# Edge stage of a two-layer graph network: ScalarE writes constants into the accumulators, a bias is moved out of the message, and edge attributes are scaled before they are turned

## The chip, the cores and the metric

The kernel runs on one core of one Trainium2 chip. The metric is the time on the device in microseconds (us), from the first to the last instruction of the core, as the median of several executions of the same program. A lower number is better.

## What is computed

The input is a graph with 50,000 nodes (128 features each) and 25,000 edges, sorted by their receiving node `dst`, with 128 attributes per edge. The reference, cut to what matters:

```python
h = maximum(layernorm(x), 0)
# layer 0 (PNA): a message per edge, four aggregates per receiving node
m = concat(h[dst], h[src]) @ W_pre.T + b_pre
mx, mn, mean, std = segment max, min, mean, sqrt(relu(var) + 1e-5) of m over dst   # 0 for nodes without edges
agg = concat(mx, mn, mean, std);  amp = log(deg + 1);  att = 1 / amp
x = x + (concat(h, agg, agg * amp, agg * att) @ W_post.T + b_post) @ W_lin.T + b_lin
# layer 1: mean of the edge attributes over the receiving node
h = maximum(layernorm(x), 0)
x = x + relu(concat(h, segment_mean(edge_attr)) @ W1 + b1) @ W2 + b2
```

## The kernel before, in words

**Two stages.** The node stage goes over all nodes in 98 chunks of 512 rows, computes every node as if it had no edges, stores the result, and writes a table of normalised rows and inputs to memory. The edge stage goes over the 25,000 edges in 49 chunks of 512, computes the nodes that do have edges, and writes only the last edge of each run of equal `dst` back over the stored row. Each stage is software-pipelined: every engine runs its own `edge_step(k)` in an order written out by hand, in which it works on chunk k ("have"), k+1 ("ahead") and k-1 ("behind"), and semaphores tie the engines together. An engine executes its own queue strictly in the written order, so a wait holds back all that is written behind it.

**Feature-major edges.** In the edge stage gathered rows are turned on TensorE, so that edges lie along the free dimension. A segmented sum, maximum or minimum is then one scan on VectorE over 512 edges, with a mask row that restarts it at each new receiver: `keep` (0 or 1, multiplied), `reset` and `lift` (added). The masks are made once, written to memory, and broadcast back to 128 partitions for each chunk by SyncE's queue.

**One edge step on each engine.**
- TensorE (PE in the profile): `turn_sender`, `layer0` for four tiles of 128 edges (L614 to L624, thirteen matmuls of up to 384 columns per tile, into the banks 5 and 6 in turn), `sender_part` (L670), `turn_receiver` (L650), `turn_normed` (L678), `turn_attr` (L661), `hidden` (L691 to L696), and `outputs`: one matmul of `ones` with `b2_rows` that puts the bias b2 into bank 7 (L701), then sixteen (by the records) with the hidden rows (L704).
- VectorE (DVE): four `mix` (L1100, L1106, L1115), five scans (L1170, L1184, L1198, L1208, L1218), the means and the variance (L1227, L1234, L1239), three `low_part` (L1122: a float32 value less its rounded high part), two more low parts (L1150, L1157), `moments`, `factors`, `outputs` (L1134).
- ScalarE (ACT): copies out of PSUM with Relu (L810, L816, L847, L865), `message` (L835: the product of `sender_part` in bank 3 plus the bias b_pre, into bank 4), its square (L841), high parts (L853), `normalise` (L824), `deviation` (L869, L873).
- GpSimd (POOL): the indirect transfers, that is, per chunk eight gathers (L444: senders `hs`, receivers `rows`, each for four tiles) and four scatters (L450); in addition three small copies of indices and factors (L397, L418, L438), three one-element additions that order the transfers (`go`, L465), and two wide operations: `receiver_const` (L406: the receiver's rows plus a constant, 128x512, into `xdc`) and `mean_attr` (L461: the running sum of attributes times 1/count, into `attr_mean`).

`attr_mean` of chunk k-1 is the operand of the first matmul of `hidden(k-1)` in TensorE's step k. SyncE loads the masks of chunk k+4 once `attr_mean` of chunk k exists.

Of the kernel before, what the change touches and what calls it, by code (L numbers as in the profile page):

```python
# [47 lines left out]
def build(nc, x, src, dst, edge_attr, w_pre, b_pre, w_post, b_post, w_lin, b_lin, w1, b1, w2, b2, out):  # L48
# [13 lines left out]
    keep_row = nc.dram_tensor("keep_row", [ROWS * RW], BF16, kind="Internal").ap()  # L62
    reset_row = nc.dram_tensor("reset_row", [ROWS * RW], BF16, kind="Internal").ap()
# [43 lines left out]
    edge_const = sb("edge_const", [P, TILES, P])  # L107
# [4 lines left out]
    PAIR, LOW = 64, 32  # L112
    ones = sb("ones", [PAIR, P], F32R)
    b2_hi = sb("b2_hi", [PAIR, CHUNK], F32R)
    b2_rows = sb("b2_rows", [PAIR, CHUNK], F32R)

    attr_mean = sb("attr_mean", [P, 2, CHUNK])
    hd_flat = attr_mean[:].rearrange("p b w -> p (b w)")  # L120
# [17 lines left out]
    inv_count = sb("inv_count", [P, RW])  # L138
    keep_sb = sb("keep_sb", [P, RW], BF16)
# [7 lines left out]
    scale = sb("scale", [P, 2, ROWS, 2])  # L147
# [36 lines left out]
    gather_go = sb("gather_go", [P, 1])  # L184
    oidx = sb("oidx", [P, 4, TILES], I32)
    amp_att = sb("amp_att", [P, 4, 2, TILES])
# [37 lines left out]
    TURNS = 4  # L224
# [31 lines left out]
    with nc.Block() as block:  # L256

        @block.sync
        def _(sp):
# [30 lines left out]
            def node_step(k, i):  # L290
                if k == 0:

                    sp.wait_ge(sem("masks_done"), 1)
                    sp.dma_start(keep_row.rearrange("(r w) -> r w", w=RW), keep_sb[0:ROWS, :]).then_inc(r, 16)
                    sp.dma_start(reset_row.rearrange("(r w) -> r w", w=RW), reset_sb[0:ROWS, :]).then_inc(r, 16)
                    sp.dma_start(lift_row.rearrange("(r w) -> r w", w=RW), lift_sb[0:ROWS, :]).then_inc(r, 16)
                    sp.dma_start(inv_row.rearrange("(r w) -> r w", w=RW), inv_count[0:ROWS, :]).then_inc(r, 16)
# [26 lines left out]
            def edge_step(k, i):  # L324
                c = k + 4
                if edge(c):
                    s = c % 4
                    if c == 0:
                        sp.wait_ge(r, 64)
                    if c >= 4:  # L330

                        sp.wait_ge(sem("e_attr_mean"), c - 3 + EU * i)
                    m = sem(f"e_masks_in{s}")
                    for dst_sb, row in ((keep, keep_row), (reset, reset_row), (lift, lift_row), (inv, inv_row)):
# [25 lines left out]
        def _(pool):  # L360
# [34 lines left out]
            def copy_scales(c, i):  # L395
                t = bass.ds(2 * c + (2 * EU) * i, 2)
                pool.tensor_copy(amp_att[:, c % 4].rearrange("p w (r h) -> p w r h", h=2), scale[:, :, t, :]).then_inc(sem("e_scale"), 1)  # L397

            def receiver_const(c, i):
                pool.wait_ge(sem(f"e_gathered{c % 4}"), 16 * 2 * TILES * (c // 4 + 1) + 16 * 2 * TILES * i)  # L400
                if c == 0:

                    pool.wait_ge(sem("n_x1"), NODE_CHUNKS)
                if c >= 2:
                    pool.wait_ge(sem("e_mixed"), TILES * (c - 1) + TILES * EU * i)
                pool.tensor_tensor(xdc[:, c % 2], xd[:, c % 4], edge_const[:], ALU.add).then_inc(sem("e_xdc"), 1)  # L406
# [13 lines left out]
            def gather_rows_of(c, i):  # L420
# [9 lines left out]
                if c >= 4:  # L430
# [5 lines left out]
                    pool.wait_ge(sem("e_xdc"), c - 3 + EU * i)  # L436
# [18 lines left out]
            def mean_attr(c, i):  # L455
                pool.wait_ge(sem("e_attr_run"), c + 1 + EU * i)
                if c >= 2:
                    pool.wait_ge(sem("e_u_psum"), 2 * (c - 1) + 2 * EU * i)
                if c < 4:
                    pool.wait_ge(sem(f"e_masks_in{c % 4}"), 64)  # L460
# [3 lines left out]
            def go():  # L464
                pool.tensor_tensor(gather_go[:], eps_col[:], eps_col[:], ALU.add)  # L465

            def edge_step(k, i):
                if edge(k + 1):
                    copy_scales(k + 1, i)
                if edge(k + 4):  # L470
                    gather_rows_of(k + 4, i)
                    pool.wait_ge(sem("e_idx"), k + 5 + EU * i)
                    go()
                    gather(k + 4, (0, 1))
                if edge(k + 1):
                    receiver_const(k + 1, i)
                if edge(k + 4):
                    if edge(k + 1):
                        pool.wait_ge(sem("e_xdc"), k + 2 + EU * i)
                        go()  # L480
                    gather(k + 4, (2, 3))
                if edge(k - 2):
                    scatter_rows_of(k - 2, i)
                    pool.wait_ge(sem("e_oidx"), k - 1 + EU * i)
                    go()
                    scatter(k - 2)
                if edge(k):
                    mean_attr(k, i)
# [6 lines left out]
        def _(pe):  # L495
# [42 lines left out]
            pe.wait_ge(sem("count_ready"), 1)  # L538
            for s in range(SCALERS):
# [3 lines left out]
            pe.wait_ge(sem("comb_h_out"), 1)  # L543

# [51 lines left out]
            def layer0(c, j, i):  # L596

                acc = bank[5 + j % 2]
                if c == 0 and j == 0:

                    pe.wait_ge(sem("n_out"), NODE_CHUNKS)
                if c == 0 and j == 1:
                    pe.wait_ge(sem("n_ut"), 2 * NODE_CHUNKS)
# [712 lines left out]
```

## Time and profile before

| | |
|---|---|
| time, median of 3 runs | 1620.67 us (1620.6 to 1627.65) |
| the profiled execution | 1626.46 us, of which the span of the core is 1624.7 us |
| TensorE busy | 1494.9 us (92% of the span) |
| VectorE busy | 1397.1 us (86%) |
| GpSimd busy | 1236.0 us (76%) |
| ScalarE busy | 939.8 us (58%) |
| mean granted TensorE clock | 0.973 of full speed |

The node stage fills the first 560 us or so, the edge stage the rest. A share of busy time is an average over both. Gaps between the instructions of an engine are not counted as busy, even where they recur before each instruction of one kind.

### The profile page before, as it was taken

How to read it: one execution, taken by the hardware profiler on the slowest of the kernel's cores; microseconds unless marked ns; L12 is line 12 of the kernel's file. 1: busy time of each engine (PE TensorE's matmuls, PEld its weight loads, DVE VectorE, ACT ScalarE, POOL GpSimd, SP SyncE). 2: the span in 40 equal slices, each digit the busy share in tenths (PEclk: the TensorE clock that was granted, in tenths of full speed). 3: DMA queues.
4: the chain of work that ended last, by engine and by line, in shares of the span. 5: the costliest groups of instructions: out<-in, count | busy, mean ns of one | idle time of the engine just before them, and what ended most of it. 6: DMA issues, size and time to landing. Idle time of an engine off the chain costs nothing.

```text
span 1624.7 us, 33700 instructions
## 1 busy us (share of the span) xinstructions
PE 1494.9 (92%) x8747; PEld 1257.4 (77%) x8747; DVE 1397.1 (86%) x4327; ACT 939.8 (58%) x1976; POOL 1236.0 (76%) x1376
## 2 busy tenths in 40 slices
PE   2899999999999759999999999999998999999995
PEld 2799998889999648888777787777777777777783
DVE  5899999999999468899888997988887888888892
ACT  1799999999999534455444453434444444444341
POOL 1778777777778777888888888888888888888833
PEclk9899999999999979999999999999999999999997
DMA  3455555555555622233233333333332323333200
GB/s 88 163 209 206 207 207 201 201 201 204 204 203 206 187 87 85 84 86 90 90 91 92 93 92 91 92 91 89 93 91 79 95 86 89 94 93 93 89 18 15
DMA packets 158898, 197.95 MB, mean 122 GB/s; under 512 B 18912, under 2 KB 115321, under 8 KB 158858
## 3 DMA queue, kind: packets, MB, share of 16 engines
q1 hardware_dynamic: 136906, 149.93, 28.3%
q0 software_dynamic: 21952, 47.55, 9.5%
q8 instruction: 17, 0.28, 0.1%
q14 instruction: 23, 0.19, 0.0%
HBM read 111.11 MB, written 90.17 MB: 124 GB/s over the span
## 4 chain that ended last, share of the span: by engine, by line
PE 82%; DVE 6%; issue 5%; ACT 3%; another core or an unknown queue 3%; DMA 1%; SPq 1%; POOL 0%; DVEq 0%; ACTq 0%; POOLq 0%
PE bank L572 12%; PE bank L621 6%; PE bank L581 6%; PE bank L614 5%; PE bank L691 5%; PE bank L618 5%; PE bank L615 5%; PE bank L624 5%; PE bank L704 5%; PE bank L670 3%; PE bank L593 3%; PE bank L591 3%; PE bank L592 3%; PE bank L555 3%
## 5 line engine op out<-in xcount | busy, mean ns | idle before, releaser
L444 POOL DMA_INDIRECT rows<-table,idx x196 | 208.3, 1063 | 59.7 <-issue 59.7
L450 POOL DMA_INDIRECT y<-nout,oidx x196 | 200.0, 1020 | 70.6 <-issue 70.3
L444 POOL DMA_INDIRECT hs<-table,idx x196 | 204.8, 1045 | 44.7 <-issue 31.2
L614 PE MATMUL bank<-comb_lo,agg_hi 128*128 128x384 f32 x588 | 212.4, 361 | 16.6 <-DVE nout L1019 10.7
L572 PE MATMUL bank<-w_sb,nut 128*128 128x128 f32 x1568 | 202.9, 283 | 5.5 <-issue 4.7
L379 POOL TENSOR_TENSOR runs<-nx,b_all 128x512 f32<-128x512 f32 x98 | 125.9, 1284 | 107.9 <-DVE nx L1029 107.8
L572 PEld LDWEIGHTS bank<-w_sb,nut 128*128 128x128 f32 x1568 | 184.5, 193 | 23.1 <-issue 14.2
L618 PE MATMUL bank<-comb_hi,agg_lo 128*128 128x384 f32 x588 | 200.1, 340 | 0.0
L615 PE MATMUL bank<-comb_hi,agg_hi 128*128 128x384 f32 x588 | 199.5, 339 | 0.0
L781 ACT ACTIVATE nh<-nx,nms,nrs 128x128 f32<-128x128 f32 x392 | 161.8, 484 | 1.1 <-DVE nms L1002 0.5
L621 PE MATMUL bank<-comb_sd,agg_sd 128*128 128x384 f32 x392 | 159.6, 489 | 0.0
L865 ACT ACTIVATE nut<-bank,b_col 128x512 f32<-128x512 f32 x98 | 67.5, 689 | 151.9 <-PE bank L696 138.4
L391 POOL TENSOR_SCALAR rows<-rows,nmv,nrs 128x128 f32<-128x128 f32 x196 | 154.6, 798 | 0.0
L388 POOL TENSOR_TENSOR xdc<-rows,lone_const 128x512 f32<-128x512 f32 x98 | 125.1, 1276 | 32.7 <-DVE nrs L1039 32.7
L691 PE MATMUL bank<-attr_mean,w_attr 128*128 128x512 f32 x196 | 111.3, 652 | 30.9 <-issue 30.2
L796 ACT ACTIVATE nut<-bank,b_col 128x512 f32<-128x512 f32 x196 | 125.6, 681 | 15.3 <-remote 11.2
L1100 DVE SCALAR_TENSOR_TENSOR part<-bank,amp_att,xdc 128x128 f32<-128x128 f32 x196 | 67.6, 345 | 75.8 <-remote 27.1
L614 PEld LDWEIGHTS bank<-comb_lo,agg_hi 128*128 128x128 f32 x588 | 111.3, 189 | 20.5 <-issue 14.8
L624 PE MATMUL bank<-comb_h_lo,hdt 128*128 128x384 f32 x196 | 125.0, 638 | 0.0
L810 ACT ACTIVATE hst<-bank 128x512 f32<-128x512 f32 x49 | 29.3, 598 | 164.2 <-PE bank L637 130.5
L615 PEld LDWEIGHTS bank<-comb_hi,agg_hi 128*128 128x128 f32 x588 | 111.6, 190 | 2.2
L618 PEld LDWEIGHTS bank<-comb_hi,agg_lo 128*128 128x128 f32 x588 | 111.1, 189 | 0.0
(180 smaller groups left out, 4196.9 us busy)
## 6 DMA issues: line engine op xcount, KB each, us to landing
table<-rows SPq DMA_DIRECT2D x98, 512.0 KB, 2.7
rows<-in_x SPq DMA_DIRECT2D x98, 256.0 KB, 3.1
y<-nout SPq DMA_DIRECT2D x98, 256.0 KB
inv<-inv_row SPq DMA_DIRECT2D x49, 256.0 KB
attr<-in_edge_attr SPq DMA_DIRECT2D x48, 256.0 KB
keep<-keep_row SPq DMA_DIRECT2D x49, 128.0 KB
reset<-reset_row SPq DMA_DIRECT2D x49, 128.0 KB
lift<-lift_row SPq DMA_DIRECT2D x49, 128.0 KB
```

The source lines that it names most:

```text
L379: pool.tensor_tensor(nx1b[:, c % 4], nx1[:, c % 2], b2_all[:], ALU.add).then_inc(sem("n_x1b"), 1)
L391: last = pool.tensor_scalar(nh[:, c % 4, j, :], nx[:, c % 4, j, :], nmv1[:, c % 4, j, 0:1], nrs1[:, c % 4, j:j + 1], ALU.subtract, ALU.mult)
L444: pool.indirect_dma_start(out=to[:, s, j, :], out_offset=None, in_=of, in_offset=bass.IndirectOffsetOnAxis(ap=idx[:, s, which, j:j + 1], a ...
L450: pool.indirect_dma_start(out=out, out_offset=bass.IndirectOffsetOnAxis(ap=oidx[:, c % 4, j:j + 1], axis=0), in_=eout[:, c % 2, j, :], in_ ...
L572: mm = pe.matmul(bank[5][:, j * P:(j + 1) * P], nut[:, c % 2, m, j * P:(j + 1) * P], w2_sb[:, m, :], start=(m == 0), stop=(m == 1))
L614: pe.matmul(acc[:, 0:SCALERS * P], hi, w_lo, start=(a == MX), stop=False, skip_group_check=True)
L615: pe.matmul(acc[:, 0:SCALERS * P], hi, w_hi, start=False, stop=False, skip_group_check=True)
L618: pe.matmul(acc[:, 0:SCALERS * P], lo, w_hi, start=False, stop=False, skip_group_check=True)
L621: pe.matmul(acc[:, 0:SCALERS * P], agg_sd[:, c % 2, cols], comb_sd[:].rearrange("p s f -> p (s f)"), start=False, stop=False, skip_group_c ...
L624: mm = pe.matmul(acc[:, 0:SCALERS * P], h[:, c % 2, cols], w[:].rearrange("p s f -> p (s f)"), start=False, stop=(w is comb_h_hi and h is ...
L691: pe.matmul(bank[b][:], w1_attr[:, cols], attr_mean[:, c % 2, :], start=True, stop=False)
L781: last = act.activation(nh2[:, b, j, :], nx1[:, b, j, :], ACT.Identity, scale=nrs2[:, b, j:j + 1], bias=nms2[:, b, j:j + 1])
```

## The change

- **Seeds.** `acc_seed` (128x384) holds all constants of layer 0. ScalarE copies it into the accumulator (bank 5 or 6) ahead of each tile (`seed`, four per chunk), and TensorE's first matmul of the tile accumulates onto it. One opening matmul per bank precedes the stage (`open_sums`). `receiver_const` and `xdc` go: `mix` reads the gathered row itself.
- **Output bias.** ScalarE copies b2 into bank 7 (`out_bias`). TensorE's matmul with `ones` goes.
- **Message.** b_pre no longer enters the message; it is multiplied by the summed weights once, in the setup, and is part of `acc_seed`. `message` on ScalarE goes; the products alternate between the banks 3 and 4, and scans and square read them there. The scans wait for the square (`e_bsq`).
- **Attributes.** ScalarE multiplies each edge's attributes by 1/count before they are turned (`scale_attr`, four 128x128 per chunk), and the scan uses a float32 mask `keepm` = (count-1)/count, so that it yields a running mean. `mean_attr` on GpSimd goes; `hidden` reads the scan's result. The new mask is one more broadcast of 256 KB per chunk.
- **Moves.** The `low_part` of the maximum moves from VectorE to GpSimd. GpSimd gathers three chunks ahead instead of four. On VectorE the receiver's low part comes first, the scans change places, and the attributes' scan goes from the middle of the step to behind the last `mix`. TensorE turns the receiver first, and the attributes one tile sooner; ScalarE has another order.

The core of the diff (conditions and the renamed counters of masks left out):

```diff
 POOL
-            def receiver_const(c, i):
-                ...
-                pool.tensor_tensor(xdc[:, c % 2], xd[:, c % 4], edge_const[:], ALU.add).then_inc(sem("e_xdc"), 1)
-            def mean_attr(c, i):
-                ...
-                pool.tensor_tensor(attr_mean[:, c % 2, :], run_attr[:, c % 2, :], inv[:, c % 4, :],
-                                   ALU.mult).then_inc(sem("e_attr_mean"), 1)
+            def low_part(a, rows, c, i):
+                pool.wait_ge(sem(f"e_hi{a}"), c + 1 + EU * i)
+                if c >= 2:
+                    pool.wait_ge(sem("e_layer0"), TILES * (c - 1) + TILES * EU * i)
+                pool.tensor_tensor(agg_lo[:, c % 2, a, :], rows, agg_hi[:, c % 2, a, :],
+                                   ALU.subtract).then_inc(sem(f"e_lo{a}"), 1)
 gather_rows_of(c, i), for c >= 4:
-                    pool.wait_ge(sem("e_xdc"), c - 3 + EU * i)
+                    pool.wait_ge(sem("e_mixed"), TILES * (c - 3) + TILES * EU * i)
 edge_step(k, i):
-    copy_scales(k + 1); gather_rows_of(k + 4); gather(k + 4, (0, 1)); receiver_const(k + 1)
-    gather(k + 4, (2, 3)); scatter(k - 2); mean_attr(k)
+    gather_rows_of(k + 3); gather(k + 3, (0, 1)); copy_factors(k + 2)
+    gather(k + 3, (2, 3)); scatter(k - 2); low_part(MX, run_max[...], k + 1)

 PE
             def layer0(c, j, i):
-                if j >= 2:
-                    pe.wait_ge(sem("e_mixed"), TILES * c + j - 1 + TILES * EU * i)
-                elif c >= 1:
-                    pe.wait_ge(sem("e_mixed"), TILES * (c - 1) + j + 3 + TILES * EU * i)
+                pe.wait_ge(sem("e_seeded"), TILES * c + j + 1 + TILES * EU * i)
-                    pe.matmul(acc[:, 0:SCALERS * P], hi, w_lo, start=(a == MX), stop=False, skip_group_check=True)
+                    pe.matmul(acc[:, 0:SCALERS * P], hi, w_lo, start=False, stop=False, skip_group_check=True)
 outputs(c, i):
-                pe.matmul(bank[7][:], ones[:], b2_rows[:], start=True, stop=False, skip_group_check=True)
+                pe.wait_ge(sem("e_b2"), c + 1 + EU * i)
 edge_step(k, i):
-    turn_sender(k + 1); layer0(k, 0); sender_part(k + 1); turn_receiver(k + 1); layer0(k, 1)
-    turn_normed(k - 1); layer0(k, 2); turn_attr(k); hidden(k - 1); layer0(k, 3); outputs(k - 1)
+    turn_receiver(k + 1); turn_sender(k + 1); layer0(k, 0); sender_part(k + 1); layer0(k, 1)
+    turn_attr(k); turn_normed(k - 1); layer0(k, 2); hidden(0, k - 1); hidden(1, k - 1); layer0(k, 3); outputs(k - 1)

 ACT
-                act.activation(bank[4][:], bank[3][:], ACT.Identity, bias=b_pre_col[:]).then_inc(sem("e_b"), 1)
+            def seed(c, j, i):
+                if c == 0 and j < 2:
+                    act.wait_ge(sem("e_sums_open"), 1)
+                elif j >= 2:
+                    act.wait_ge(sem("e_mixed"), TILES * c + j - 1 + TILES * EU * i)
+                else:
+                    act.wait_ge(sem("e_mixed"), TILES * (c - 1) + j + 3 + TILES * EU * i)
+                act.activation(bank[5 + j % 2][:, 0:SCALERS * P], acc_seed[:], ACT.Copy).then_inc(sem("e_seeded"), 1)
+            def scale_attr(c, i):
+                ...
+                for j in range(TILES):
+                    last = act.activation(attr[:, c % 2, j, :], attr[:, c % 2, j, :], ACT.Copy,
+                                          scale=factor[:, c % 4, 2, j:j + 1])
+            def out_bias(c, i):
+                act.wait_ge(sem("e_ut"), 2 * c + 1 + 2 * EU * i)
+                act.activation(bank[7][:], b2_all[:].rearrange("p j f -> p (j f)"), ACT.Copy).then_inc(sem("e_b2"), 1)
 edge_step(k, i), after:
+    seed(k, 1); sender_turned(k + 1); receiver_turned(k + 1); spread(k - 1); message_squared(k + 1)
+    normalise(k - 1); seed(k, 2); normed_turned(k - 1); mean_squared(k + 1); high_part(MX, k + 1)
+    hidden(0, k - 1); seed(k, 3); hidden(1, k - 1); high_part(ME, k + 1); out_bias(k - 1)
+    high_part(MN, k + 1); seed(k + 1, 0); variance_pos(k + 1); deviation(k + 1); scale_attr(k + 1)

 DVE edge_step(k, i), after:
+    outputs(k - 2); factors(k - 1); receiver_low(k + 1); mix(k, 0); scan_sum(k + 1); scan_max(k + 1)
+    message_mean(k + 1); normed_low(k - 1); mix(k, 1); scan_squares(k + 1); scan_min(k + 1)
+    square_mean(k + 1); mix(k, 2); variance(k + 1); low_part(ME); low_part(MN); mix(k, 3)
+    scan_attr(k); moments(k)
```

The setup gains the mask `keepm`, the product of b_pre with the summed weights, the two instructions that make `acc_seed`, and a reciprocal of the turned factors (98 edge half-rows by two); it loses the splitting of b2 and one reciprocal of 98x256.

## Rows read from the trace of the kernel before

**Rows 1.** The page: busy time of each engine, its share of the span, instructions.

```profile
PE 1494.9 (92%) x8747; PEld 1257.4 (77%) x8747; DVE 1397.1 (86%) x4327; ACT 939.8 (58%) x1976; POOL 1236.0 (76%) x1376
```

**Rows 2.** Busy us of each engine by stretch; then granted clock, DMA share, GB/s.

```profile
976.00:1520.00 544.00, 507.77 (x2584) 409.01 (x2585) 455.77 (x951) 239.54 (x456) 445.46 (x512) 0.98 0.32 91
1529.80:1581.00 51.20, 51.02 (x257) 41.28 (x258) 46.42 (x97) 21.76 (x41) 24.55 (x28) 0.97 0.14 42
```

**Rows 3.** The two longest waits of GpSimd, 640 to 1520 us: in total, times, longest.

```profile
POOL y L450 <- issue: 60.8, 168, 0.6
POOL rows L444 <- issue: 50.9, 167, 0.3
```

**Rows 4.** Timeline of GpSimd: the first instruction of four of its edge steps.

```profile
626.24 0.65 POOL L397 COPY amp_att<-scale 128x8 f32<-128x8 f32 x1
...
668.54 0.22 POOL L397 COPY amp_att<-scale 128x8 f32 x1
...
688.04 0.24 POOL L397 COPY amp_att<-scale 128x8 f32 x1
...
1529.80 0.21 POOL L397 COPY amp_att<-scale 128x8 f32<-128x8 f32 x1
```

**Rows 5.** Waits of TensorE, 640 to 1520 us.

```profile
PE bank L691 <- issue: 28.2, 18, 2.2
PE bank L678 <- ACT nh L824: 15.8, 14, 2.0
```

**Rows 6.** Groups of GpSimd, 640 to 1520 us: count, busy, mean ns, idle before.

```profile
L444 POOL DMA_INDIRECT rows<-table,idx x167 | 179.8, 1077 | 50.9 <-issue 50.9
L444 POOL DMA_INDIRECT hs<-table,idx x167 | 176.4, 1056 | 37.4 <-issue 25.3
L461 POOL TENSOR_TENSOR attr_mean<-runs,inv 128x512 f32<-128x512 f32 x42 | 54.6, 1300 | 0.4
L406 POOL TENSOR_TENSOR xdc<-rows,edge_const 128x512 f32<-128x512 f32 x42 | 54.4, 1294 | 0.7
```

**Rows 7.** Timeline of TensorE near the end: the bias matmul of two steps.

```profile
1556.83 0.49 PE L701 MATMUL bank<-b_rows,ones 64*128 64x512 f32 x1
1557.25 2.05 PE L704 MATMUL bank<-w_sb,nut 128*128 128x128 f32 x16
...
1575.99 0.49 PE L701 MATMUL bank<-b_rows,ones 64*128 64x512 f32 x1
```

**Rows 8.** Timeline of VectorE and of GpSimd: instructions of both at once.

```profile
1017.57 2.06 DVE L1227 TENSOR_TENSOR mean_b<-runs,inv 128x512 f32<-128x512 f32 x1
1017.78 1.29 POOL L461 TENSOR_TENSOR attr_mean<-runs,inv 128x512 f32<-128x512 f32 x1
...
1042.15 0.69 DVE L1239 TENSOR_TENSOR var<-var,mean_b 128x512 f32<-128x512 f32 x1
1042.25 1.51 POOL L444 DMA_INDIRECT hs<-table,idx  x1
```

**Rows 9.** Groups of ScalarE, 640 to 1520 us.

```profile
L824 ACT ACTIVATE nh<-nx,ms,rs 128x128 f32<-128x128 f32 x168 | 68.9, 486 | 0.0
L835 ACT ACTIVATE bank<-bank,b_pre_col 128x512 f32<-128x512 f32 x42 | 27.8, 662 | 100.1 <-PE bank L670 87.2 <-issue 9.2 <-remote 3.8
```

**Rows 10.** Group of VectorE, 640 to 1520 us.

```profile
L1122 DVE TENSOR_TENSOR agg_lo<-runs,agg_hi 128x512 fp32r<-128x512 f32 x86 | 62.8, 770 | 0.0
```

**Rows 11.** TensorE's end of a tile, and VectorE's first reading of it.

```profile
1074.83 0.34 PE L624 MATMUL bank<-comb_h_hi,hdt 128*128 128x384 f32 x1
...
1076.96 0.35 DVE L1100 SCALAR_TENSOR_TENSOR part<-bank,amp_att,xdc 128x128 f32<-128x128 f32 x1 [3.16 <-remote]
```

**Rows 12.** Timeline of TensorE: one of its waits on `hidden`.

```profile
1061.82 1.15 PE L691 MATMUL bank<-attr_mean,w_attr 128*128 128x512 f32 x2 [2.08 <-issue]
```

**Rows 13.** The stretch that begins there, with the columns of Rows 2.

```profile
1061.80:1066.60 4.80, 4.78 (x10) 2.85 (x11) 4.66 (x7) 0.69 (x1) 4.27 (x5) 0.64 0.45 140
```

**Rows 14.** Timeline of VectorE in the setup: the reciprocal that goes.

```profile
23.37 1.70 DVE L963 RECIPROCAL runs<-runs 98x256 f32<-98x256 f32 x1
```

More of the change, by code:

```diff
@@ L538, in _ @@
             pe.wait_ge(sem("count_ready"), 1)
+            pe.matmul(bank[6][:, P:(1 + SCALERS) * P], b_pre_wide[:], part_sum[:].rearrange("p s f -> p (s f)"),
+                      start=True, stop=True)
             for s in range(SCALERS):
@@ L626, in layer0, with open_sums @@
                 mm.then_inc(sem("e_layer0"), 1)
+            def open_sums():
+                pe.wait_ge(sem("n_out"), NODE_CHUNKS)
+                pe.wait_ge(sem("n_ut"), 2 * NODE_CHUNKS)
+                for acc in (bank[5], bank[6]):
+                    mm = pe.matmul(acc[:, 0:SCALERS * P], ident[:], comb_sd[:].rearrange("p s f -> p (s f)"),
+                                   start=True, stop=True, skip_group_check=True)
+                mm.then_inc(sem("e_sums_open"), 1)
             def turn_sender(c, i):
@@ L676, in turn_normed @@
                     pe.wait_ge(sem("e_h2l"), c + EU * i)
+                if not last:
+                    pe.wait_ge(sem("e_hst"), c + 3 + EU * i)
                 for j in range(TILES):
@@ L875, in edge_step @@
             def edge_step(k, i):
-                ahead, behind = edge(k + 1), edge(k - 1)
+                have, ahead, behind = edge(k), edge(k + 1), edge(k - 1)
+                if k == 0:
+                    seed(0, 0, i)
+                if have:
+                    seed(k, 1, i)
                 if ahead:
                     sender_turned(k + 1, i)
+                    receiver_turned(k + 1, i)
                 if behind:
@@ L881, in edge_step @@
                 if ahead:
-                    message(k + 1, i)
-                    receiver_turned(k + 1, i)
+                    message_squared(k + 1, i)
                 if behind:
                     normalise(k - 1, i)
-                if ahead:
-                    message_squared(k + 1, i)
+                if have:
+                    seed(k, 2, i)
                 if behind:
@@ L1264, in edge_step @@
                     factors(k - 1, i)
+                if ahead:
+                    receiver_low(k + 1, i)
                 if have:
@@ L1278, in edge_step @@
                     scan_squares(k + 1, i)
+                    scan_min(k + 1, i)
                     square_mean(k + 1, i)
-                    variance(k + 1, i)
-                if have:
-                    scan_attr(k, i)
-                if ahead:
-                    low_part(MX, run_max[:, (k + 1) % 2, :], k + 1, i)
-                    low_part(MN, run_min[:, (k + 1) % 2, :], k + 1, i)
                 if have:
```

244 lines of the change are left out of this document (126 added, 118 removed).

## The prediction

> **What bounds the kernel now.** I read the page first [rows 1]: TensorE is busy for 92% of the span, which makes it the suspect. The change is in the edge stage, so I asked for the busy time by stretch [rows 2]. From 976 to 1520 us TensorE is busy for 507.8 of 544 us, VectorE for 455.8, GpSimd for 445.5, ScalarE for 239.5. GpSimd's 82% looks harmless. Its waits say otherwise [rows 3]: from 640 to 1520 us it waits for nothing but "issue", never over 0.6 us, about 0.3 us ahead of each transfer. Those gaps belong to the transfers, so GpSimd is never idle for want of work. Its timeline gives the pace [rows 4]: from the first of these starts to the last are 43 steps, (1529.80 - 626.24) / 43 = 21.01 us each.
>
> TensorE does wait [rows 5]: 28.2 us in 18 waits ahead of `hidden`, whose operand `attr_mean` GpSimd makes, and 15.8 us in 14 waits for `normalise`. The wait of 2.08 us before 1061.82 [rows 12] ends at the moment GpSimd's wide operation does. What TensorE can do unhindered stands near the end, when no gathers are left: 1575.99 - 1556.83 = 19.16 us a step [rows 7]. So GpSimd at 21.0 us sets the pace, TensorE at 19.2 us comes next. VectorE has 455.8 / 544 x 21.3 (the mean step in that stretch, by GpSimd's starts) = 17.8 us of work, ScalarE by the same sum 9.4.
>
> **The change part by part, per edge step.**
>
> GpSimd. `receiver_const` goes: 54.4 / 42 = 1.30 us [rows 6]. `mean_attr` goes, another 1.30 us, and `low_part` of the maximum comes, the same kind of operation (two 128x512 inputs, one output); I give it the same 1.30 us. Twelve transfers and the small copies stay; the copy of factors has twelve elements a row for eight, nothing that shows. Sum: 21.01 - 1.30 = 19.7 us. The unknown is how much of the 21.01 is mutual hindrance with VectorE. A gather takes 1.06 to 1.08 us on the mean [rows 6], and 1.51 us where a VectorE operation on two buffers runs beside it [rows 8]. The quickest step of all took 688.04 - 668.54 = 19.5 us [rows 4], so hindrance is worth 1.5 us of the mean step. One such VectorE operation leaves VectorE (the low part), the order of the rest changes. Bounds for GpSimd: 19.5 - 1.3 = 18.2 us with next to no hindrance; above, 20.2 us, one third more hindrance than now. I take 19.7, the hindrance as it is, since that quickest step stands alone among the 43.
>
> A rule of the Trainium skill bears on this (SBUF — State Buffer, "Who interferes with whom"): a VectorE instruction with two inputs in SBUF contends with a GpSimd instruction that reads SBUF, and the later one waits until the first is through. The trace agrees for wide operations: `mean_b` took 2.06 us beside GpSimd's 1.29 us [rows 8], against the 0.69 us that a like operation, `variance`, takes in the same rows. By the same section such an operation should not hold up the making of descriptors; the 1.51 us of the gather [rows 8] speaks against that. By the rule alone GpSimd would come near the lower bound, and the pace would be TensorE's.
>
> TensorE. The bias matmul of `outputs` goes: 1557.25 - 1556.83 = 0.42 us [rows 7], so 19.16 - 0.42 = 18.74 us. Nothing else leaves it. This is its best case. In many steps its work ends later than recorded: a tile ends at 1075.17, VectorE could read it at once and starts at 1076.96 [rows 11], 1.8 us late, where others start 0.2 us behind the recorded end. Over 45 steps the extra lateness at this place has a mean of 0.7 us, from 0 to 2.4; if TensorE truly spends it, it needs 19.4 us. That still fits under 19.7.
>
> VectorE. One `low_part` goes, 0.77 us [rows 10], two wide GpSimd operations become one beside it. 17.8 becomes 17.0 us. `mix` costs the same with the gathered row. Not the pace.
>
> ScalarE. Out: `message`, 0.66 us. In: four seeds (128x384; between 0.49 for 128x128 and 0.66 for a 128x512 that is written into a bank [rows 9], so 2.0 to 2.6 us), `out_bias` 0.66, `scale_attr` four like `normalise`'s, 68.9 / 42 = 1.64 us. Sum: 9.4 - 0.66 + 4.3 to 4.9, up to 13.6 of 19.7 us. Not the pace, but it now stands between VectorE and TensorE: `layer0` waits for a seed where it waited for `mix`. I walked through a step with TensorE's durations, t = 0 at `turn_receiver`. Tile 0 ends at 3.7, the sender's product at 4.6, the square at 5.3, `normalise` at 7.0, seed 2 at 7.5; TensorE wants them at 7.8 and 8.3. `hidden(0)` is copied by 13.4, seed 3 done at 13.9, wanted at 14.2. The bias is in bank 7 at 16.2, wanted at 17.0. Everything fits, seed 3 with 0.3 us. What slips is covered by 19.7 - 18.74 = 0.96 us of slack a step; with the cover gone each us slipped costs a us.
>
> New waits. `low_part(MX, k+1)` is GpSimd's last item in step k and gates `layer0(k+1, 0)`. In the other direction GpSimd's step k waits for chunk k-1 to be mixed. The loop runs over two steps: from the gate 15.8 us of TensorE to the end of tile 3, 1.1 us of `mix`, 19.7 us of GpSimd, 36.6 in all, 18.3 a step, below the pace. Behind GpSimd's wait stand gathers needed two steps later, and scatters. If it fails, `low_part` is late next, and with it the whole of TensorE's step. With a lead of three chunks a gather still has over a step to land. SyncE queues five mask loads for four, one of them 256 KB, behind a wait for the attributes' scan; they are needed three steps later, and DMA engines are 32% busy [rows 2]. The attributes of chunk k+2 queue behind them and have some 17 us. I cost both at nothing.
>
> Outside the steady part. Start: the first `mix` results no longer wait behind low parts, about -3 us. The last four steps, in which TensorE leads: 4 x 0.42 = -1.7. Setup: a reciprocal of 98x256 goes (1.70 us [rows 14]), the splitting of b2 goes beside TensorE's work, and `acc_seed`, a reciprocal of about 1.3 us and a matmul come ahead of the node stage; I take +2.5 (bounds 0 and +4). The node stage is untouched.
>
> Sum: 43 x (21.01 - 19.7) = 56.3, + 3 + 1.7 - 2.5 = 58.5 us less. The profiled execution would fall from 1626.5 to 1568; it lies 5.8 us above the median of the runs, so for the median 1620.7 - 58.5 = 1562 us.
>
> **The rivals.**
>
> (a) *TensorE sets the pace.* Hindrance on GpSimd nearly vanishes in the new order, GpSimd needs 18.2 us. TensorE's best is 18.74, say 18.9: 43 x 2.11 = 91, + 2.2 = 93 less, 1528 us. For it: the quickest GpSimd step, and TensorE steps of 19.16 us. Against: the mean gather is well above its shortest, and TensorE's lateness of 0.7 us. The skill's section named above speaks for it.
>
> (b) *GpSimd was not what held TensorE.* Its unbroken row is what it takes up when TensorE is slow for reasons of its own (lateness, or the clock: behind the 2.08 us wait the granted clock was 0.64 over 4.8 us [rows 12, 13]). Then only the matmul is saved, 0.42 x 49 = 20.6 us: 1600 us. For it: some TensorE steps take 23 us although its waits in them are 2 us. Against: GpSimd has no wait.
>
> (c) *The change does not do what it says:* ScalarE's handoffs eat the gain. If seeds and bias come late by a mean 1.5 us a step, TensorE needs 18.74 + 0.7 + 1.5 = 20.9, 4.7 us less over 43 steps, and 2.2 outside: 1614 us, no change that can be told. Against: the walk through a step above.
>
> (d) *Slower.* TensorE waits for seed 2 and seed 3 each step, 0.5 us each, and its clock falls once a step. The fall cost 0.36 x 4.8 = 1.7 us in [rows 13]. 18.74 + 1.0 + 1.7 = 21.4 us, 43 x 0.4 = 17 more: 1638 us. It decides once waits and falls exceed 21.01 - 18.74 = 2.27 us a step. For it: seed 3 has 0.3 us of slack. Against: a single wait of 2 us was needed for the fall before, and some such waits had none behind them.
>
> **How the numbers follow.** The forecast (GpSimd at 19.2 to 20.2 us a step, 1541 to 1584 us) has a chance of 0.56. (a) 0.12, (b) 0.17, (c) 0.08, (d) 0.07. A difference of 0.5%, 8 us, is about what a measurement of this kernel can tell from none. Below 1612.6: the forecast, (a) and nearly all of (b), 0.84. Within: the rest of (b) and (c), 0.09. Above 1628.8: (d), 0.07. The predicted time is 1562 us. The range, 1530 to 1604, takes in the forecast, most of (a) and (b), and leaves out (c) and (d).
>
> **What would show it.** GpSimd's starts 19.7 us apart and still without waits but "issue"; if it waits for `mix` or for the high part, TensorE has taken over (a). TensorE's waits move from `hidden` to the third matmul of tile 0, which needs GpSimd's low part; if they stand ahead of the first matmul of tiles 2 or 3, released by ScalarE, (c) or (d) holds. L701 is gone, and `sender_part`, tiles and `hidden` keep their durations. ScalarE's busy time a step rises to 13 to 14 us, VectorE's falls by some 0.8. In the setup TensorE's first node matmul comes 0 to 4 us later than at 40.6 us. The prediction is wrong if GpSimd's gathers stretch more than before with the new order of scans, if ScalarE's copies into a bank cost much more than its copies out of one, or if TensorE's unexplained lateness was what set the pace.

## The result: 9.3% slower where it was measured, 5.7% faster in other series

The changed kernel took 1782.47 us (median of 4 runs, 1770.21 to 1784.44) against 1620.63 us for the kernel before (4 runs, 1619.68 to 1627.65): the ratio is 1.093, 95% interval 1.0835 to 1.1027. A further run of it is on record with 1757.25 us. I had predicted 1562 us, range 1530 to 1604, and 0.84 for faster. On that measurement the prediction is wrong.

That number can't be understood without this: in a later series the same file, unedited, took a median of 1535.21 us (4 runs, 1534.34 to 1535.57) against 1627.55, ratio 0.943, interval 0.9414 to 0.9446. The kernel before shows no such jump (medians 1620 to 1631 throughout). A series is a set of kernels run one after another on one chip (a "call" in the expectations). I name the two conditions *late* (TensorE's signals come late) and *prompt*; all runs of a series agreed. The result and series 1, 3 and 6 were late, 2, 4 and 5 prompt; series 1 and 2 had the same chip, 23 minutes apart (there I know the condition from edited kernels, since the unedited one was in neither).

The page's busy time, of the changed kernel, in the late condition and then in the prompt one:

```profile
PE 1519.1 (86%) x8704; PEld 1270.6 (72%) x8704; DVE 1338.9 (76%) x4275; ACT 1060.3 (60%) x2368; POOL 1114.7 (63%) x1329
```
```profile
PE 1451.2 (95%) x8704; PEld 1242.0 (81%) x8704; DVE 1311.9 (86%) x4275; ACT 1057.9 (69%) x2368; POOL 1137.0 (74%) x1329
```

The sums move by 5% at most, so the time is in waits. One stretch of the edge loop, late, by windows (the columns are those of [rows 2]), then its waits:

```profile
640.00:1440.00 800.00, 678.19 (x3338) 543.64 (x3336) 562.89 (x1200) 398.64 (x866) 491.62 (x637) 0.94 0.31 89
```
```profile
engine line waited for: us in total, times, longest us
ACT nh2t L846 <- remote: 168.6, 31, 6.8
POOL idx L437 <- DVE nx L1148: 165.9, 32, 8.2
...
PE bank L697 <- issue: 92.7, 33, 3.8
...
ACT bsq L840 <- remote: 63.8, 15, 4.7
...
PE bank L605 <- ACT bank L873: 13.7, 12, 2.8
```

and the same stretch, prompt:

```profile
640.00:1440.00 800.00, 790.42 (x4225) 659.09 (x4224) 682.79 (x1516) 502.13 (x1099) 637.36 (x803) 1.00 0.39 114
```
```profile
ACT nut L864 <- PE bank L701: 130.1, 84, 2.6
ACT bsq L840 <- PE bank L672: 117.6, 42, 3.3
...
ACT nh2t L846 <- PE bank L682: 48.7, 43, 1.2
```

Late, 3338 TensorE rows fit into 800 us; prompt, 4225 do. GpSimd no longer sets the pace in the late condition: it waits 5 us a step for the mix. What leads there is the wait of ScalarE's copy of h2, the normalised rows that TensorE has turned (nh2t), 5.4 us a time, and its releaser is "remote": at the moment of release no recorded instruction ends. Prompt, TensorE and GpSimd are nearly level. GpSimd waits for "issue", as in [rows 3], and for the mix only 3.0 us in all, and TensorE's third matmul of tile 0 waits for GpSimd's low part in every step, at its weight load and in some steps at the matmul:

```profile
POOL y L449 <- DVE nx L1148: 3.0, 10, 0.3
PEld bank L609 <- POOL agg_lo L459: 23.0, 42, 1.0
PE bank L609 <- POOL agg_lo L459: 7.5, 11, 0.7
```

One step shows the wait for h2. Late:

```profile
1138.14 0.66 PE L682 MATMUL bank<-ident,nh 128*128 128x128 f32 x4 [0.58 <-issue]
...
1144.74 2.07 PE L697 MATMUL bank<-runs,w_attr 128*128 128x512 f32 x2 [3.19 <-issue]
```
```profile
1137.99 0.48 ACT L873 ACTIVATE bank<-acc_seed 128x384 f32<-128x384 f32 x1
1143.92 0.60 ACT L846 ACTIVATE nh2t<-bank 128x512 fp32r<-128x512 f32 x1 [5.45 <-remote]
```

Prompt, L682 is recorded at 1116.43 for 0.60 us, and then

```profile
1117.15 0.60 ACT L846 ACTIVATE nh2t<-bank 128x512 fp32r<-128x512 f32 x1 [1.18 <-PE bank L682]
```

The turn ends in the record at 1138.80 and its reader starts 5.12 us later; prompt it is 0.12. I call this difference the lag. Over the 49 chunks its median is 4.9 us (44 over 1 us) against 0.04 (none). Late steps are mostly 22 to 26 us, from the third one on; prompt ones 18.8, and 19.5 once per turn of the loop, by the 0.7 us that TensorE then waits for the low part.

The last four chunks are the exception, in every late run of the changed kernel and its variants: there the lag is 0.04 us. It goes with the gathers. The last gather starts at 1671.1 us, the next copy of h2 is 5.1 us late (the first row below), and the one after it is on time, although TensorE has no pause from 1684 us on:

```profile
1674.89 0.60 ACT L846 ACTIVATE nh2t<-bank 128x512 fp32r<-128x512 f32 x1 [6.20 <-remote]
1693.37 0.60 ACT L846 ACTIVATE nh2t<-bank 128x512 fp32r<-128x512 f32 x1 [1.10 <-issue]
```
```profile
1662.00:1684.00 22.00, 18.90 (x89) 14.65 (x87) 14.65 (x35) 10.41 (x23) 13.93 (x18) 0.92 0.40 112
1684.00:1703.00 19.00, 19.00 (x108) 16.20 (x107) 17.04 (x38) 12.31 (x27) 5.61 (x7) 1.00 0.08 25
```

### The profile page after: what moved, and what is told of

The parts are those of the page before. It is cut to its first block, busy times and chain, and to the rows that moved or that the text cites. A ratio compares the mean times of both kernels' runs of the same rounds, so it can differ in the third digit from the quotient of the medians.

```text
span 1768.4 us, 34450 instructions
## 1 busy us (share of the span) xinstructions
PE 1519.1 (86%) x8704; PEld 1270.6 (72%) x8704; DVE 1338.9 (76%) x4275; ACT 1060.3 (60%) x2368; POOL 1114.7 (63%) x1329
## 4 chain that ended last, share of the span: by engine, by line
PE 72%; issue 12%; another core or an unknown queue 5%; ACT 5%; DVE 3%; POOL 1%; DMA 0%; SPq 0%; ACTq 0%; DVEq 0%; POOLq 0%
PE bank L571 11%; PE bank L697 6%; PE bank L612 5%; PE bank L580 5%; PE bank L605 5%; PE bank L615 4%; PE bank L609 4%; PE bank L606 4%; PE bank L709 4%; PE bank L590 3%; PE bank L592 3%; PE bank L591 3%; PE bank L554 2%; PE bank L562 2%
## 5 line engine op out<-in xcount | busy, mean ns | idle before, releaser
L449 POOL DMA_INDIRECT y<-nout,oidx x196 | 207.3, 1058 | 73.0 <-issue 72.7
L697 PE MATMUL bank<-runs,w_attr 128*128 128x512 f32 x196 | 140.2, 806 | 120.7 <-issue 120.7
L605 PE MATMUL bank<-comb_lo,agg_hi 128*128 128x384 f32 x588 | 227.9, 388 | 18.3 <-ACT bank L873 18.3
L443 POOL DMA_INDIRECT rows<-table,idx x196 | 190.9, 974 | 60.8 <-issue 60.8
L443 POOL DMA_INDIRECT hs<-table,idx x196 | 191.3, 976 | 53.3 <-issue 45.9
L1190 DVE SCALAR_TENSOR_TENSOR nh2l<-bank,nh2t 128x512 fp32r<-128x512 f32 x49 | 33.9, 692 | 213.9 <-issue 116.0
L846 ACT ACTIVATE nh2t<-bank 128x512 fp32r<-128x512 f32 x49 | 29.3, 597 | 239.1 <-remote 220.1
L437 POOL COPY idx<-index 128x8 int32 (+1 forms) x49 | 9.9, 201 | 234.6 <-DVE nx L1148 234.6
L697 PEld LDWEIGHTS bank<-runs,w_attr 128*128 128x128 f32 x196 | 44.2, 246 | 141.4 <-issue 134.1
```

Source lines behind the costliest of these rows:

```text
L443: pool.indirect_dma_start(out=to[:, s, j, :], out_offset=None, in_=of, in_offset=bass.IndirectOffsetOnAxis(ap=idx[:, s, which, j:j + 1], a ...
L449: pool.indirect_dma_start(out=out, out_offset=bass.IndirectOffsetOnAxis(ap=oidx[:, c % 4, j:j + 1], axis=0), in_=eout[:, c % 2, j, :], in_ ...
L605: pe.matmul(acc[:, 0:SCALERS * P], hi, w_lo, start=False, stop=False, skip_group_check=True)
L697: pe.matmul(bank[b][:], w1_attr[:, cols], run_attr[:, c % 2, :], start=True, stop=False)
```

## The experiments

Each ratio is to the kernel before in the same series, with its interval. Across series only what is far outside the intervals is compared.

**Series 1 (late): is it the clock, the DMA burst, or ScalarE's order?** fill:

```
+ for _ in range(8):   # in hidden(0), ahead of the wait for h2t
+     pe.matmul(bank[7][:, 0:SCALERS * P], comb_sd[:, 0, :], comb_sd[...], start=True, stop=True)
```

> The changed kernel with eight extra 128x384 matmuls into bank 7 ahead of the wait for h2t (they add about 8 x 0.17 = 1.4 us of work to each of the 49 steps and their result is overwritten, so nothing is left out). Theory A, the idle waits of TensorE are real, its clock falls after them and the low clock makes the next wait: the fillers lie inside the wait of 2.85 us, the clock stays up, h2t's lag of 5.0 us shrinks, and a step takes at most 22 us, 1700 us or less. Theory B, the array is not idle in that wait, it works off a backlog that its recorded times do not show: the fillers come on top, a step takes 1.4 us more, 1830 to 1850 us, and the lag does not shrink.

1823.88 us, ratio 1.124 (1.114 to 1.1345). The clock in the records stays up and TensorE's record is nearly full, and yet nothing is won, and h2t is as late as before (median lag 5.1 us):

```profile
640.00:1440.00 800.00, 778.32 (x3763) 608.57 (x3763) 544.86 (x1160) 384.33 (x839) 474.48 (x619) 1.00 0.31 87
```

Theory A falls: the low recorded clock after waits is not the cause. Theory B is only half borne out. The time stays 6 us below its range, and the median step is 24.5 us against 23.8 in the result's profile (another series), so the fillers cost about 0.7 us of their 1.4. masks_later exchanges SyncE's mask and attr blocks:

```
+ sp.wait_ge(sem("e_h2t"), c - 3 + EU * i)   # with the masks' other waits; attr's block now goes first
```

> The changed kernel with SyncE's two blocks of a step exchanged: attr first, and the five mask loads wait for h2t too, so that their burst (1.15 MB, 8 us) no longer lies over layer0(k,1) and the turn of h2 but over hidden and layer0(k,3), where the kernel before has it. Theory C, the burst slows TensorE or its signals in that stretch: h2t's lag of 5.0 us goes to below 1.5 and the time to 1650 or less. Theories A and B (clock, or order of ScalarE's work): the lag stays at 4 to 6 us and the time within 2% of 1780.

1757.04 us, ratio 1.083 (1.067 to 1.099), the median lag is 4.4 us: not theory C. seed3_early:

```
- if behind:
-     hidden(0, 7, k - 1, i)
  if have:
      seed(k, 3, i)
  if behind:
+     hidden(0, 7, k - 1, i)
      hidden(1, 1, k - 1, i)
```

> The changed kernel with ScalarE's seed(k,3) ahead of the copy of hidden(0) instead of behind it. Theory D, the handoffs of ScalarE cost the time: TensorE's wait for a seed (16.7 us in 15 of the 41 steps) goes, and since such a wait feeds the lower clock, a step falls by 1 us or more, 1740 or less. If the lag of h2t is the cause and not the seeds: 1765 to 1785, and h2t's lag stays at 5 us.

1734.84 us, ratio 1.069 (1.059 to 1.080). The wait for a seed is gone, the large one stays (before the edit, 92.7 and 13.7):

```profile
PE bank L697 <- issue: 85.0, 31, 3.8
PE bank L682 <- ACT nh L832: 7.9, 6, 1.5
```

The time lies within theory D's bound of 1740, but the lag is still 4.5 us. The seed's place may be worth something in the late condition. How much is open, as the unedited kernel was not in this series. It isn't the cause of the lag. before_noconst:

```
- receiver_const(k + 1, i)        # and the mix reads xd; gathers k + 3 ahead instead of k + 4
```

> The kernel before with one part of the change alone: GpSimd does not add the constant (receiver_const is left out, the mix reads the gathered rows, and the constant is missing from the output), and the gathers lead by three chunks as in the changed kernel. My prediction's premise, GpSimd sets the pace of the kernel before: a step goes from 21.0 us by the 1.3 us to 19.7, 1560 to 1575 us. Rival, GpSimd only keeps up with a loop through the other engines: 20.5 us a step or more, 1600 to 1625 us, and GpSimd waits for the mix.

1678.99 us, ratio 1.035 (1.017 to 1.053): less work on GpSimd and slower. Its steps run at 19.2 us, up to seven in a row, and between them come one to five of 20 to 27. So even the kernel before falls into the lateness (42 of 49 h2t signals over 1 us) with this edit. It took the constant away and shortened the lead at once, and the lead alone (before_lead3, below) was run only in the prompt condition: that TensorE's missing pauses bring the lateness about, and not the shorter lead, is argued.

**Series 2 (prompt, which I didn't know).** marks_after makes SyncE a witness:

```
+ def mark(name, signal, count):
+     sp.wait_ge(sem(signal), count)
+     sp.dma_start(marks[name][...], ident[0:1, 0:4]).then_inc(sem(f"marked{k % 4}"), 16)
```

> The changed kernel with SyncE as a witness: after each of ten signals of TensorE in a step (the four tiles, the message, the three turns, the two hidden parts, the outputs) it issues a 16-byte DMA, so the trace shows when that signal really came; SyncE's step loop is written out for it. Nothing is left out. Theory E, the array itself is late: from layer0(k,1) on all signals are late by the same growing amount, layer0(k,1)'s and turn_attr's as much as the turn of h2 (4 to 5 us), and the tiles' signals are further apart than their recorded 3.0 us. Theory F, only ScalarE is late or only that one signal: the mark of the turn of h2 comes within 1 us of its recorded end, or the marks before and after it do. The time stays within 2% of 1780 us.

1534.21 us, ratio 0.943 (0.9375 to 0.948): not a witness of anything late, but 250 us less than expected.

> The kernel before with the gathers three chunks ahead instead of four and nothing else changed (GpSimd still adds the constant). Theory G, what made the kernel without the constant slower is that TensorE then runs at its own 19.2 us a step without a pause and is held up for 6 to 9 us every few steps: here GpSimd still gives the pace of 21.0 us and the time stays at 1620 to 1635. Theory H, it is the shorter lead of the gathers (their DMAs beside others, GpSimd's wait for the mix): 1660 to 1690 here too.

1626.72 us, ratio 0.9986 (0.997 to 1.0002). In the prompt condition the shorter lead costs nothing.

> The kernel before without the constant (as before_noconst), and the four masks of an edge chunk are loaded for the first four chunks only and then used again (masks of other chunks, so the output is another one): 640 KB less DMA in each of the other 45 steps, the same instructions on the engines. Theory C', the mask burst is what holds TensorE up: the steps of 24 to 28 us go, all take 19.2 to 19.7 us, 1560 to 1575 us. Theory G, a TensorE without pauses is held up whatever the DMA does: 1660 to 1680 as with the masks.

1547.69 us, ratio 0.951 (0.946 to 0.956). TensorE has no pause at all and every step is 19.2 us, the pace of [rows 7]:

```profile
640.00:1440.00 800.00, 800.00 (x4215) 659.04 (x4214) 704.04 (x1540) 396.98 (x756) 652.10 (x754) 1.00 0.22 65
```

> The changed kernel with its five masks loaded for the first four chunks only (masks of other chunks afterwards, so the output is another one), 896 KB less DMA a step. Theory C', the burst holds TensorE up: h2t's lag goes below 1.5 us and the step to 19 to 20 us, 1560 to 1600 us. Otherwise the lag stays at 4 to 5 us and the time at 1720 to 1780.

1535.9 us, ratio 0.944 (0.939 to 0.949). I read series 2 as proof that the mask loads, or SyncE's way of issuing them, held TensorE up. That was wrong; the control was missing.

**Series 3 (late).** after_written and before_written write SyncE's edge loop out; masks_spread puts waits for the message and for h2t between its mask loads.

> The changed kernel with SyncE's loop over the edge steps written out, so its DMAs have constant addresses and its waits constant values; the same DMAs in the same order, behind the same waits, and no marks. Theory I, the way SyncE issues the mask loads inside its loop is what holds TensorE up (there the last of them are issued in 0.01 to 0.19 us each instead of 0.43): the time is that of the kernel with marks, 1530 to 1545 us, steps of 18.8 us. Theory J, the marks did it (they spread SyncE's small DMAs over the step or keep it awake): 1740 to 1780 us as the changed kernel.

1799.05 us, ratio 1.102 (1.095 to 1.1095): theory I falls.

> The kernel before with the same edit, SyncE's loop over the edge steps written out. Theory I and GpSimd as the pace: a step stays at 20.5 to 21.2 us, 1600 to 1625 us. If GpSimd was itself held up by the mask loads: the steps go to TensorE's 19.2 us, 1545 to 1555 us. Theory J: no change, 1618 to 1628.

1631.08 us, ratio 1.0002 (0.996 to 1.0044).

> The changed kernel, loop kept, with its mask loads in three portions: keep and reset at once, lift and inv behind the message of the next step, keepm and attr behind h2t. The same bytes and instructions. Theory K, it is the load of the DMA engines at its peak (1.0 for 3 to 4 us): with portions of 256 to 512 KB h2t's lag falls below 2 us and the time below 1650. Theory I, the loop's form of issue: the lag stays and the time is 1740 to 1790.

1825.73 us, ratio 1.121 (1.1145 to 1.1281), with a median lag of 5.9 us: theory K falls too. The prompt run moves more in the same stretch (114 GB/s against 89 late, in the windows above) and is not late.

**Series 4 (prompt): the control.**

> The changed kernel itself, unedited, beside the kernel with marks on one chip: the control for what the marks, and the left out mask loads, were given credit for. Theory L, the marks do something: 1760 to 1790 us here and 1530 to 1545 us with marks. Theory M, what differs is not in the kernel but in the chip or the moment that it is run on: both come out alike, either near 1535 or near 1780.

> The kernel with marks, unedited, on the same chip as after_again. Theory L: 1530 to 1545 us, steps of 18.8 us, every signal of TensorE within 0.1 us of its recorded end. Theory M: the same time as after_again within 1%.

1535.21 and 1534.33 us: theory M. In the prompt condition the marks do nothing, and leaving out the mask loads in series 2 had done nothing either.

**Series 5 (prompt).** paced adds two adds on GpSimd ahead of low_part:

```
+ for n in range(2):
+     pool.tensor_tensor(nxc[:, n], b2_all[:], lone_const[:], ALU.add)
```

> The kernel with marks once more, as control and as witness: so far each call found its chip in one of two conditions, one in which the changed kernel takes 1535 us and one in which it takes 1760 to 1800. If this call finds the second, the marks show when each of TensorE's signals really comes. Theory E, the array is late as a whole: layer0(k,1), the turn of attr and the turn of h2 are late one after another by 1 to 5 us, and the gaps between them are up to twice their recorded 2.9 and 0.5 us. Theory F, one signal alone is late: its neighbours come within 0.1 us of their recorded ends. In the first condition: 1534 us and nothing late.

> The changed kernel with masks loaded for the first four chunks only (another output), on the same chip as marks_third. If the condition is the slow one: 1535 to 1560 us if the mask burst is part of what makes TensorE late there, 1700 to 1780 if not. If it is the other: 1536 again, and nothing is learnt.

> The changed kernel with two adds of 1.28 us more on GpSimd in each step, ahead of its low_part (their result is never read), so that TensorE has about 1.5 to 2 us of pause in a step as in the kernel before. First condition: GpSimd gives the pace, 20.3 to 21.3 us a step, 1605 to 1650 us. Slow condition: if it takes a TensorE without pauses to bring the lateness about, 1610 to 1660 here too, much faster than the changed kernel; if it takes only the order of the work, h2t's lag is 4 to 5 us and the time 1780 or more.

1534.62, 1534.03 and 1666.63 us (ratio 1.0225, 1.016 to 1.029), paced worse than I expected. TensorE then waits for GpSimd, once in most steps, and its steps lie mostly between 19.4 and 25.1 us, for a long stretch in alternation (the waits from 640 to 1600 us):

```profile
PE bank L611 <- POOL agg_lo L459: 90.1, 34, 4.2
```

What the pause does in the late condition was not run.

**Series 6 (late): the witness works.**

> The kernel with marks again, as control and witness, for the case that this call finds the chip in the slow condition (three of six calls did). Slow: 1700 us or more, and the marks show whether layer0(k,1), the turn of attr and the turn of h2 are late together (the array is behind) or one alone. Other condition: 1534 us and nothing late.

> The changed kernel with masks for the first four chunks only (another output), beside marks_fourth. Slow condition: 1535 to 1560 us if the mask burst is needed for the lateness, 1700 or more if not. Other condition: 1535 us.

1766.95 us, ratio 1.086 (1.073 to 1.099), and 1746.57 us, ratio 1.0735 (1.054 to 1.093). With no mask loads after the first four chunks the lateness is nearly all there (median lag 4.45 us, against 4.9 with them):

```profile
ACT nh2t L846 <- remote: 176.3, 33, 7.0
```

So the mask loads are not needed for it; the two medians are 20 us apart. The marks of one step (SyncE issues each as soon as the signal is there; in order tile 0, message, tile 1, turn of attr, turn of h2, tile 2, and the two parts of hidden in one row; tile 3 and the outputs left out here), prompt in marks_third:

```profile
960.45 0.24 SPq L330 DMA_DIRECT2D mark_layer<-ident  x1
961.25 0.24 SPq L330 DMA_DIRECT2D mark_message<-ident  x1
963.98 0.21 SPq L330 DMA_DIRECT2D mark_layer<-ident  x1
964.42 0.21 SPq L330 DMA_DIRECT2D mark_attr<-ident  x1
964.86 0.21 SPq L330 DMA_DIRECT2D mark_normed<-ident  x1
967.59 0.21 SPq L330 DMA_DIRECT2D mark_layer<-ident  x1
969.14 1.77 SPq L330 DMA_DIRECT2D mark_hidden<-ident  x2
```

and late in marks_fourth, with what TensorE's rows say of the same signals:

```profile
1095.01 0.23 SPq L330 DMA_DIRECT2D mark_layer<-ident  x1
1095.66 0.23 SPq L330 DMA_DIRECT2D mark_message<-ident  x1
1102.88 0.21 SPq L330 DMA_DIRECT2D mark_layer<-ident  x1
1104.32 0.21 SPq L330 DMA_DIRECT2D mark_attr<-ident  x1
1105.76 0.21 SPq L330 DMA_DIRECT2D mark_normed<-ident  x1
1108.78 0.21 SPq L330 DMA_DIRECT2D mark_layer<-ident  x1
1109.58 2.29 SPq L330 DMA_DIRECT2D mark_hidden<-ident  x2
```
```profile
1097.93 0.34 PE L643 MATMUL bank<-comb_h_hi,hdt 128*128 128x384 f32 x1
1098.11 0.60 PE L689 MATMUL bank<-ident,attr 128*128 128x128 f32 x4
1098.55 0.60 PE L710 MATMUL bank<-ident,nh 128*128 128x128 f32 x4
...
1101.54 0.33 PE L643 MATMUL bank<-comb_h_hi,hdt 128*128 128x384 f32 x1
1106.61 1.66 PE L725 MATMUL bank<-runs,w_attr 128*128 128x512 f32 x2 [4.73 <-issue]
...
1108.92 0.63 PE L729 MATMUL bank<-nh2l,w_hi 128*128 128x512 f32 x1
```

The rows have tile 1 done at 1098.27 and the turn of h2 at 1099.15; their signals come at 1102.88 and 1105.76, 4.6 and 6.6 us later. The signals are late one after another: between message and tile 1 lie 7.22 us here and 2.73 prompt, between the turns 1.44 and 0.44. So it is not one signal alone (theory F falls), and TensorE's rows do not show it. Up to here that is what theory E, the array itself is late, forecast. The next two signals do not fit it. Tile 2's comes at 1108.78, 6.9 us after its row's end (1101.87), and that of hidden's first part at 1109.58, just when its own last row ends (1109.55). An array that finished tile 2 only at 1108.78 would have had 0.8 us left for matmuls that take 1.55 us prompt. So, if the array works in the written order, tile 2's signal came later than its work. Whether the array is slow, or finished work is signalled late, the runs leave open. Windows of marks_fourth, from the message to tile 1's mark and from there to the turn's:

```profile
1095.01:1102.88 7.87, 6.87 (x38) 5.74 (x36) 3.96 (x6) 2.50 (x6) 5.86 (x10) 1.00 0.66 222
1102.88:1105.76 2.88, 0.00 (x0) 0.00 (x0) 0.00 (x0) 0.00 (x0) 2.27 (x3) 1.00 0.11 36
```

In the second no matmul is recorded, and the signals of the two turns, four transposes each, come in. Mean gaps over the steps 3 to 46, in us, worked out from the marks:

```
                 prompt (44 steps)   late (44 steps)
message->tile 1        2.73               5.95
->turn of attr         0.44               0.99
->turn of h2           0.44               1.05
->tile 2               2.73               3.83
tile 2->hidden 0       1.55               0.66
hidden 0->tile 3       4.32               4.40
tile 3->outputs        1.78               1.76
median step           18.78              23.8
```

From hidden 0 on a step is alike. Up to the turn of h2 the signals come at less than half the prompt pace (2.73 to 5.95, 0.44 to 1.05), in tile 2 at 0.7 of it, and the step is 5.0 us longer. The gap from tile 2 to hidden 0 is shorter than its matmuls take prompt; in 24 of the 44 late steps it is 0.26 us, the time SyncE needs from one mark to the next, so hidden's signal was there as soon as tile 2's had been marked.

## Why the prediction was right or wrong, point by point

- **GpSimd sets the pace of the kernel before** [rows 3, 4]: borne out in the prompt condition. Without its constant the steps fall to TensorE's 19.2 us (noconst_still), with it they stay at 21.2 (before_lead3). The first of the two also had the masks of four chunks only; in the changed kernel that made no difference prompt (1535.9 and 1534.2 us).
- **GpSimd's 21.01 - 1.30 = 19.7 us** was the term that I took for the new pace. It is mis-sized: prompt, the mean step is 18.95 us (42.2 steps in 800 us), and GpSimd keeps up. The gaps ahead of its transfers stayed: from 640 to 1440 us it has 3.8 us a step without an instruction before and 3.9 after. Its busy time fell from 654.04 us in 38.1 steps to 637.36 in 42.2, 17.2 to 15.1 a step, 2.1 us and not 1.3. The rest lies in its small instructions: the one-element additions took 0.34 us in the mean before and 0.20 prompt, the copies of factors 0.53 and 0.20, those of indices 0.35 and 0.20, some 0.9 us a step. So of the hindrance that I had left "as it is" about half of the 1.5 us went, if these stretches are hindrance; 18.95 is inside my bounds for GpSimd, 18.2 to 20.2. The sign that I named came too: TensorE waits at the third matmul of tile 0 for the low part.
- **TensorE's 19.16 - 0.42 = 18.74 us** measured 18.8 prompt (with 19.5 once per turn of the loop, where it waits for GpSimd). My rival "TensorE sets the pace", 1528 us at a chance of 0.12, is nearly what happens there: 1535. That number lies in my range of 1530 to 1604, but outside the 1541 to 1584 of the forecast itself; it got there by the mis-sized term above.
- **ScalarE's additions** fit: seeds 0.48 us, output bias 0.59, scaled attributes 0.39 each in the prompt profile, and TensorE does not wait for a seed there. Its busy time a step is 502.13 / 42.2 = 11.9 us, less than the 13 to 14 that I forecast. "Everything fits, seed 3 with 0.3 us" holds in the prompt condition; late, seed 3 is waited for 12 times in 800 us, 13.7 us.
- **The step that failed** is the term for TensorE's lateness. I took the recorded end of a matmul for the moment at which its result is there, gave the rest 0.7 us a step, and so had TensorE need 18.74 to 19.4 us, under GpSimd's pace, with 0.96 us of slack for what slips. In the condition of the measurement the signals in the middle of a step came 4.9 us late in the median (up to 6.6 in the step shown), the copy of h2 and `hidden` behind it had to wait for them, and a step took 23.8 us for the same instructions. The signs were there and I booked them as 0.7 us of unexplained lateness: the mix that starts late and is released by "remote" [rows 11]. The profile of before had itself been taken late, by its lag: over 1 us for 19 of 49 h2t signals, for 24 of 49 in before_written, late, and for none in before_lead3, prompt. The h2t waits of before and of before_lead3:

```profile
ACT nh2t L847 <- remote: 31.7, 14, 2.9
```
```profile
ACT nh2t L847 <- PE bank L678: 14.1, 39, 0.4
```

- **The slower rival** (TensorE waits for seeds, its clock falls, 21.4 us a step, 1638, chance 0.07) had the sign and not the mechanism. fill kept the recorded clock at 1.00 and lost; the waits for seeds are 13.7 of the 122 us that TensorE waits from 640 to 1440 us. It fell 144 us short.
- **Why the kernel before is spared**: this is argued, not shown. GpSimd's 21.0 to 21.2 us leave TensorE 2 us a step, so a small lateness is absorbed (at most 2.7 us). before_noconst, with fewer pauses, is hit. Pauses alone are not the whole of it: once the gathers have ended, TensorE runs without a pause and without lag in the same late runs.
- **Open**: what makes the signals late. The condition is not in the kernel (the same file does both), it does not need the mask loads or SyncE's loop, and it does not touch the node stage: TensorE's 40 to 560 us are busy 508.40 us late and 509.57 prompt. Within a late run the lag ends with the gathers. The rival that no run tests is therefore that the gathers, by their transfers or by GpSimd's work on them, are needed for it; a late run with gathers for the first chunks only would tell. They can't be the whole cause, since the prompt runs have the same gathers. What else the chip was doing in a late series is not on record.

The Trainium skill's "TensorE: Matmul & The Clock Gate", section "Seeing it yourself", warns that the recorded clock events can be unreliable on this chip and that the gate has been seen stuck at a quarter. The marks neither confirm nor exclude this: the granted clock reads 1.00, the 2.4 GHz level, while the signals of the two turns are 1.44 us apart and not 0.44, but a slow clock alone would not bring hidden's signal 0.8 us behind tile 2's. No run here shows what gate was in force.

## What to carry to other kernels

Read TensorE by its readers: the start of the instruction that its signal releases, less the recorded end, over many steps. Where that lag reached microseconds here and the releaser was "remote", the signals came later than the rows say, no reader could start before them, and the step length read from the rows was no floor. Look also at where the lag begins and ends within one run. Run the unedited kernel in the same series as its experiments; a ratio to another kernel doesn't reveal a condition that hits only one of the two. And this change is worth 5.7% in one condition of the chip and costs about 9% in the other: measure such a change in several series before it replaces a kernel that holds 1620 to 1631 us in all.

## What the runs showed of the hardware that I hadn't expected

- The same program took 1535 or 1782 us, within 1.6% inside a series, and one chip had both conditions (series 1 and 2, by edited kernels).
- TensorE's rows can run 6.6 us ahead of its signals, with the granted clock at 1.00; in a window without any row the signals of eight transposes came in.
- The lag ended within one step of the last gather, from 5.1 to 0.04 us, with TensorE busy for 19.00 of 19 us.
- Neither the mask loads nor the recorded clock go with the lateness: still_third, without the loads, has its h2t signals 4.45 us late in the median, and fill, at a granted clock of 1.00, 5.1 us.
